# A graph network kernel in which each node's edge from itself is no longer gathered

## The reference

```python
for l in range(3):                                    # block 0
    xr = jnp.einsum('nd,rde->rne', x, W_rel[l])       # a table: 8 rows for each node
    agg = jax.ops.segment_sum(xr[edge_type, src], dst, num_segments=N)
    x = jax.nn.relu(agg + x @ W_root[l] + bias[l])
h = x @ Wv + bv                                       # block 1
q, k = h @ wq + bq, h @ wk + bk
e = q[src] + k[dst]
c = jnp.where(e > 0, e, 0.2 * e)
attn = softmax of c over the edges of each dst
out = jax.ops.segment_sum(h[src] * attn[:, None], dst, num_segments=n)
```

## Time and profile before

| | |
|---|---|
| median of 3 runs | 4654.57 us (4651.98 to 4656.97) |
| the profiled execution's own time | 4648.88 us |
| its span, first to last instruction | 4647.1 us |
| TensorE matmul busy | 3549.5 us, 76% |
| GpSimd busy | 3227.2 us, 69% |
| ScalarE busy | 1997.3 us, 43% |
| VectorE busy | 1198.7 us, 26% |
| indirect DMAs | 3328 = 4 x 832 |

### The profile page before, as it was taken

The page is one execution under the profiler, slowest core; times in us unless marked ns, Lnnn a source line. Parts: engine busy times, 40 slices in busy tenths (PEclk is TensorE's granted clock), DMA queues, the critical chain, the costliest instruction groups (busy, mean ns, idle before and its releaser), DMA issues.

```text
span 4647.1 us, 52438 instructions
## 1 busy us (share of the span) xinstructions
PE 3549.5 (76%) x12856; PEld 2444.5 (53%) x12856; DVE 1198.7 (26%) x3972; ACT 1997.3 (43%) x5249; POOL 3227.2 (69%) x3465
## 2 busy tenths in 40 slices
PE   9997888888887888888887666666664777777767
PEld 4444655555554555555554444444443665656656
DVE  2330000000000000000000111111112777777776
ACT  2334545454443444445453434434342444444444
POOL 1126777777775777777775777777776777777775
PEclk9998999999998999899998888888877888888888
DMA  5445545454544444444443444444443444444443
GB/s 201 183 176 162 166 156 166 156 167 156 163 160 137 160 151 159 151 152 158 150 159 122 119 116 117 118 116 118 117 118 97 112 114 113 114 113 113 113 113 88
DMA packets 233747, 643.65 MB, mean 139 GB/s; under 512 B 61158, under 2 KB 106663, under 8 KB 215028
## 3 DMA queue, kind: packets, MB, share of 16 engines
q0 software_dynamic: 160336, 439.40, 33.3%
q10 hardware_dynamic: 43128, 128.52, 7.5%
q1 hardware_dynamic: 29996, 72.34, 4.3%
HBM read 466.54 MB, written 173.49 MB: 138 GB/s over the span
## 4 chain that ended last, share of the span: by engine, by line
POOL 67%; issue 22%; PE 10%; DMA 1%; DVE 0%; SPq 0%; ACT 0%; ACTq 0%; DVEq 0%; POOLq 0%
POOL ring L482 67%; PE bank L1217 8%; DMA ring<-table,code 1%; PE sum_ps L1301 0%; PE sum_ps L1421 0%; PE turn_ps L1206 0%; DMA table<-stage 0%; DMA bias_row<-in_L_gnn_bias_dram 0%; PE bank L1377 0%; DVE stage L652 0%; DMA ring<-h_table,code 0%; PE bank L1371 0%; DVE masks L880 0%; DMA h_table<-stage 0%; SPq L532 0%
## 5 line engine op out<-in xcount | busy, mean ns | idle before, releaser
L482 POOL DMA_INDIRECT ring<-table,code x2496 | 2367.5, 949 | 861.6 <-issue 787.1
L1301 PE MATMUL sum_ps<-ring,masks 128*128 x5586 | 1531.3, 429 | 711.2 <-SPq L592 661.7
L1301 PEld LDWEIGHTS sum_ps<-ring,masks 128*128 128x128 f32 x5586 | 1148.7, 213 | 1058.2 <-issue 890.7
L1217 PE MATMUL bank<-wide,xT 128*128 128x512 f32 (+1 forms) x2744 | 1141.2, 570 | 9.3 <-DMA bias_row<-in_L_gnn_bias_dram 4.4
L482 POOL DMA_INDIRECT ring<-h_table,code x832 | 791.8, 952 | 272.3 <-issue 272.3
L1069 ACT ACTIVATE masks<-node_row,local 128x128 f32<-128x128 f32 x2793 | 830.8, 387 | 22.7 <-issue 13.2
L1217 PEld LDWEIGHTS bank<-wide,xT 128*128 128x128 f32 x2744 | 527.5, 194 | 573.9 <-issue 553.7
L979 ACT COPY stage<-bank 128x512 f32<-128x512 f32 x441 | 256.8, 583 | 953.5 <-PE bank L1217 953.3
L1421 PE MATMUL sum_ps<-ring,stage 128*128 x1862 | 505.6, 420 | 0.1
L970 ACT ACTIVATE xT<-turn_ps 128x256 f32<-128x256 f32 x196 | 75.4, 385 | 815.2 <-PE turn_ps L1206 812.3
L1421 PEld LDWEIGHTS sum_ps<-ring,stage 128*128 128x128 f32 x1862 | 382.0, 217 | 52.1 <-issue 0.5
(11 more groups left out here) (141 smaller groups left out, 1454.6 us busy)
## 6 DMA issues: line engine op xcount, KB each, us to landing
table<-stage ACTq DMA_DIRECT2D x96, 1024.0 KB, 4.5
table<-stage SPq DMA_DIRECT2D x48, 1024.0 KB, 4.1
ring<-table,code POOLq DMA_INDIRECT x2496, 2.8
ring<-h_table,code POOLq DMA_INDIRECT x832, 2.8
h_table<-stage ACTq DMA_DIRECT2D x49, 130.0 KB, 2.4
features<-xT SPq DMA_DIRECT2D x49, 128.0 KB, 4.0
first_T<-features ACTq DMA_DIRECT2D x49, 128.0 KB, 4.7
wide<-in_L_gnn_W_rel_dram SPq DMA_DIRECT2D x6, 1024.0 KB, 6.2
```

Of the source, the lines that this page charges most:

```text
L482: pool.indirect_dma_start(slot(c % RING, width), None, table, bass.IndirectOffsetOnAxis(ap=code[:, c:c + 1], axis=0)).then_inc(landed[n % ...
L1217: last = nc.tensor.matmul(bank[q][:, 0:width], xT[:, b, k, :], weights[:, k, 512 * q:512 * q + width], start=(k == 0), stop=(k == K - 1))
L1301: last = nc.tensor.matmul(sum_ps[b][:, 0:D], masks[:, b, s, :], at_offset(slots[s]), start=(s == 0 and l > 0), stop=(s == SLOTS - 1))
```

## The change

**The list.** The edges are laid out as 128 runs of 832, one in each partition. VectorE finds in each run the last loop of each node, takes it out, and closes the gaps: each kept edge is packed into one word with the number of places that it must move, and six steps `move_up` move words by 1, 2, 4, ... 32 places. Each run keeps 792 places, so the list has 792 chunks where it had 832, and a tile reads 18 gathered slots. The kept lists go to DRAM and come back as chunks. The loops' types are drawn out of each run by seven steps `take_loops` (8 at a time), and put in order by 56 small matmuls after the last tile of the stage.

With the reference's inputs a run keeps at most 787 edges, and has at most 52 loops (56 fit). The tiles' edges lie in at most 18 chunks, so the general path is not taken. Tile 47 begins at chunk 760; before, it began at chunk 798.

**Layers.** A node's loop adds the row of its own type from the table. The change adds it with VectorE, by 8 multiply-adds a tile, each with a 0 or 1 for each node. For layers 1 and 2 they read the PSUM banks right after `transform`. For layer 0 the tile's table rows (1 MB) are loaded back from DRAM.

**Attention.** The tile's own rows of `h_table` are loaded by a plain DMA (`own_rows`) and take the place of a 19th slot (`HELD` = 19).

```diff
+    RUN = -(-E // (16 * P)) * 16
+    KEPT = -(-(RUN - N // P + 5) // 8) * 8
+    NCH = KEPT
...
+    MEAN = -(-(E - N) * P // N)
     SLOTS = -(-(MEAN + P) // P) + 1
+    HELD = SLOTS + 1
...
+        FIRST_CLOSING = 4 if PAIRS >= 20 else 1
+        FIRST_STEP = 20 if PAIRS >= 20 else 2 * PAIRS
...
+        def place(after, half=0):
+            return min(FIRST_STEP + 2 * after + half, 2 * PAIRS)
...
             def evacuate(l, i, use, b, first=False):
                 q = R // 2 - 1
+                if not first:
+                    add_loops(l, i, use, b, range(0, R - 2))
                 dve.wait_ge(transformed[b], CREDIT + NB * use + q + 1)
                 dve.wait_ge(stored[b], table_stored(l, b, use))
                 nc.vector.tensor_copy(stage[:, b, 512 * q:512 * (q + 1)], bank[q][:, :]).then_inc(evacuated[q], 1)
...
+                add_loops(l, i, use, b, range(R - 2, R))
...
+            def add_loops(l, i, use, b, types):
+
+                for t in types:
+                    if t % 2 == 0 and t // 2 < R // 2 - 1:
+                        settle(dve, CREDIT + l * NT + i + 1)
+                        dve.wait_ge(evacuated[t // 2], CREDIT + l * NT + i + 1)
+                    if t:
+                        settle(dve, loops_done((l - 1) * NT + i, t))
+                        dve.wait_ge(root_step, loops_done((l - 1) * NT + i, t))
+                    nc.vector.scalar_tensor_tensor(root[:, i, :], bank[t // 2][:, t % 2 * D:(t % 2 + 1) * D], loop_weight(i, t),
+                                                   root[:, i, :] if t else bias_row[:, :], ALU.mult, ALU.add
+                                                   ).then_inc(root_step, 1)
+
+            def add_first_loops(i, j, b):
+
+                dve.wait_ge(back_loaded[b], 16 * (j + 1))
+                for t in range(R):
+                    if t:
+                        settle(dve, loops_done(i, t))
+                        dve.wait_ge(back_step, loops_done(i, t))
+                    nc.vector.scalar_tensor_tensor(root[:, i, :] if t == R - 1 else loop_ps, back[:, b, t * D:(t + 1) * D],
+                                                   loop_weight(i, t), loop_ps if t else root[:, i, :], ALU.mult, ALU.add
+                                                   ).then_inc(back_step, 1)
...
+            def load_back(i, b):
+                if not isinstance(i, int) or i > 1:
+                    settle(act, loops_done(i - 2, R))
+                    act.wait_ge(back_step, loops_done(i - 2, R))
+                act.dma_start(back[:, b, :], tables_by_node[0][bass.ds(i * P, P), :]).then_inc(back_loaded[b], 16)
...
+            def load_own(i, b):
+                act.dma_start(own_rows[:, b, :], h_table[bass.ds(i * P, P), :]).then_inc(own_loaded[b], 16)
...
             def transform(step, use, b, banks, first=False, lead=False, between=None):
...
                     pe.wait_ge(evacuated[q], CREDIT + step)
+                    if not first and q < R // 2 and not lead:
+                        pe.wait_ge(root_step, loops_done(step - NT - 1, 2 * q + 2))
...
             def next_table(l, i, j, b, upcoming=None):
 
+                if l == 0 and (not isinstance(i, int) or i < NT - 2):
+                    settle(pe, loops_done(i + 1, R))
+                    pe.wait_ge(back_step, loops_done(i + 1, R))
```

More of the change, by code:

```diff
@@ L60, in gnn_program, with slots_of, gathered @@
     RINGS_PAST = CH // RING
-    def slots_of(c):
-        return range(GROUP * c, min(GROUP * (c + 1), SLOTS))
+    def slots_of(c, end=HELD):
+        return range(GROUP * c, min(GROUP * (c + 1), end))
+    def gathered(c):
+        return slots_of(c, SLOTS)
     def uses(g):
@@ L397, in _ @@
             pool.wait_ge(ranges_ready, 2)
+            step(pool.tensor_scalar(most, most, -1.0, None, ALU.add))
             step(pool.tensor_tensor(meets, per_chunk(most), per_tile(tile_base[:, 0:NT]), ALU.subtract))
@@ L445, in _ @@
             pool.wait_ge(dst_ready, 2)
[L446 to L449 removed]
+            for first in range(0, NT, AT_ONCE):
+                end = min(first + AT_ONCE, NT)
+                _, begins = nc.values_load_multi_w_load_instructions(
+                    starts[0:1, first:end], engines=[pool.engine], min_val=0, max_val=CH - SLOTS,
+                    skip_runtime_bounds_check_because="first chunks, clamped where they are computed")
+                for i in range(first, end):
+                    pool.tensor_copy(local[:, i, 0:SLOTS], dst_T[:, bass.ds(begins[i - first], SLOTS)]
+                                     ).then_inc(prep_step, 1)
             steps[0] += NT
             pool.wait_ge(prep_step, steps[0])
[L452 to L453 removed]
+            step(pool.tensor_scalar(local[:, 0:NT, 0:SLOTS], local[:, 0:NT, 0:SLOTS], far_shift[:, 0:1], None, ALU.add))
+            step(pool.tensor_tensor(local[:, 0:NT, 0:SLOTS], local[:, 0:NT, 0:SLOTS],
                                     tile_base[:, 0:NT].unsqueeze(2).to_broadcast([P, NT, SLOTS]), ALU.subtract))
@@ new lines, in _ @@
+            takings = tuple(lambda k=k: take_loops(k) for k in range(LOOPS // 8))
+            before_layers_at(tile_before_layers, (
+                (SOME // 2 * 2, from_here_later), *((closing(k), step) for k, step in enumerate(closings)),
+                (place(0), chunk_ranges), (place(1), keep_code),
+                (place(1), count_below), *((place(2 + k // 2, k % 2), step) for k, step in enumerate(takings)),
+                (place(6), any_broken), (place(7), read_loops), (place(10), plan_sums)))
@@ L1180, in attend @@
                         exponentials(b, c)
+                    if c == 1 and not last and store:
+                        settle(act, pieces_done(L, i - 1))
+                        act.wait_ge(added, pieces_done(L, i - 1))
+                        load_own(i + 1, 1 - b)
                     if c >= 2:
@@ L1207, in turn, with transform @@
                 last.then_inc(turned[b], 1)
-            def transform(step, use, b, banks, first=False, between=None):
+            def transform(step, use, b, banks, first=False, lead=False, between=None):
                 found = None
```

407 lines of the change are left out of this document (293 added, 114 removed).

## The result

The changed kernel took **4587.44 us** (median of 4 runs, 4580.98 to 4592.06), the kernel before 4653.66 in the same session: ratio 0.9859, 95% interval [0.9847, 0.9871]. It is faster, by 1.4% and not by 4.0, and 4587 lies outside the forecast range. The profiled execution took 4585.81 us, its span is 4584.1.

A forecast was written before the change was run, and what follows sets the result against it. GpSimd's own gather pace was taken as the bound. Span: 4647.1 - 200.7 (gathers) + 1 (transfers) - 1.2 (gaps) + 15 (preparation) = 4461 us; adding 1.8 and 5.7 gave 4468 us, -4.0%, range 4452 to 4500.

The forecast's parts named there:

- Can the others follow?: Layers and attention: other engines keep up with 20.3 us a tile; in attention VectorE needs 15.2 and waited 4.2.
- The plan's own term: Preparation: L448's 57.8 us shrink to 25, from 49 copies and 7 loads of 1.5; cost nothing.
- attention does not follow: Rival, attention: a chain from largest score to weights and back keeps the tile at 21.3 us; 4518 us, chance 5%.
- Gathers removed: All four passes: 40 of 832 gathers fewer in each, 160 x 1.2546 us, -200.7 us.
- VectorE and TensorE in the layers: Pass 0: VectorE 9.8 us and TensorE 17.4 us a tile fit into 20.3; the adds cost TensorE nothing.
- TensorE's bank waiting for the adds: Sign of a wrong forecast: TensorE's first bank is held until VectorE's adds are over; no size given.
- Stage before the layers, +15: Before the layers: preparation steps over 2.4 us ahead of the norm hold TensorE's turn, +15 us, bounds 8 to 34.
- The plan ready in time: Before the first gather: the plan is ready some 34 us before the table is stored, so it costs nothing.
- Gaps, -1.2: Three gaps between passes: two slots of 0.43 us drop out, up to 0.5 us of late copies enter; -0.4 each.
- The gaps start from the same place: Ends of passes: the last chunk tile 47 needs is the 13th from the end in both lists.
- The last 32.04 us stay: After the last gather: the time stays 32.04 us, since attention keeps 19 slots.
- The rule weighed there: Layer 0: VectorE instructions with two SBUF inputs contend with GpSimd's SBUF reads; up to 21 us; milder contention rival, 4489.

The follow-up runs named there:

- with the load repaired: The changed kernel with plan rows 24 words apart in place of 23 and all 24 words loaded: 4476.34 us, ratio 0.9622.

## Why the prediction was wrong

- **The step that failed** is "Can the others follow?", its line on attention. I took VectorE's 740.53 us as 15.2 a tile, set 20.3 beside it, and wrote of the 4.2 us of waiting that "one microsecond less is there to take". The register load stood in no term of the sum, and it went from 1.60 to 5.15 us in three tiles of four. That a row shrinks from 96 to 92 bytes follows from the diff (`SLOTS`, with `PLAN = SLOTS + PIECES` in the kernel), and the 1.60 us were in the trace of before; what a start off 16 bytes costs was in no row of it. (The plan's own term does price such loads, seven of GpSimd's at 1.5 us; they took 1.61 in the median.) Nor were the 4.2 us all spare. Against them the loop had to take 1.0 us from the shorter gathers and 3.55 from the load, 4.55 in all, which would miss by 0.35 us a tile; the tiles came out at 22.4 us on the mean, 2.1 above 20.3. VectorE's loop without the slow load is 23.7 - 3.55 = 20.15 us (worked out), so before it had 21.3 - 20.15 = 1.15 us to spare and not 4.2: where no row is late, VectorE waits for ScalarE instead (136.1 us for 22.6). The pass came out 108 us above the forecast.
- **The rival that came true in name** was "attention does not follow" at 5%. Its mechanism, a chain that stays at 21.3 us, was not what happened, and its bound was wrong: I let the pass keep its length at worst, and it grew by 58 us, because the loop itself grew. The loop of 20.15 us fits into 20.3 with next to nothing spare, as the first repair (rows of 24 words, 23 loaded) shows.
- **Gathers removed**: right. Interval 1.25 us, 950 and 957 ns, and with the load repaired the four passes took 994.39, 988.54, 992.13 and 998.28 us, where "about 991" was said; attention's stayed 7 us above. What the load of the table rows took of pass 0 (1 us said) was not separated; that pass is 6 and 2 us longer than the other two.
- **VectorE and TensorE in the layers**: right in what they cost. The window of pass 0 gave VectorE 441.03 us of 975, 9.2 a tile where 9.8 was said, and TensorE 17.8 where 17.4 was. With adds narrowed or not, the passes stay. One sign that the prediction had named for being wrong, TensorE's bank waiting for the adds, does stand in the profile of the changed kernel, and it is the register load again: in all 39 cases TensorE's own load (5.4 us, in two of them 3.9) is over only 0.17 us before the matmul, as in the second and third line here, and with loads of 1.6 us (the run with 24 words loaded, last line) 3.2 us remain.

```profile
PE bank L1497 <- DVE root L781: 78.0, 39, 2.8
498.62 2.05 PE L1497 MATMUL bank<-wide,xT 128*128 128x512 f32 x2 [2.50 <-DVE root L781]
L334 PEldq TENSOR_LOAD <-plan x1: 5444/5444/5444, 493.0 to 493.0; - x1
PE bank L1500 <- DVE root L784: 3.2, 2, 1.7
```

- **Stage before the layers, +15**: 17.7 measured. The mechanism (a step over 2.4 us ahead of the norm holds the turn) was right; moving the steps behind the norm gave back 17.5 (384.62 to 367.08). The prices of the forms that the trace of before lacked came out close, except the scan, 1.88 us:

```profile
L889 DVE MAX8 loop_code<-masks 128x8 f32<-128x832 f32 x7 | 7.1, 1019 | 0.0
...
L891 DVE MATCH_REPLACE8 masks<-loop_code,masks 128x832 f32<-128x832 f32 x6 | 6.0, 1008 | 0.0
...
L867 DVE TENSOR_SCALAR masks<-masks 128x832 int32<-128x832 int32 x6 | 3.5, 586 | 0.0
L832 DVE TENSOR_TENSOR_SCAN masks<-masks 128x832 f32<-128x832 f32 x1 | 1.9, 1883 | 0.0
```

- **The plan ready in time**: right, its lead was 38.91 us (34 said).
- **Gaps, -1.2**: +1.7 measured. The first gap grew by 2.2. A likely reason, which no run tried by itself: TensorE now reaches the end of pass 0 later against the gathers. Before, the last tile but one's bank copy started 3.5 us before the last gather, with the load repaired 0.6 us before it (1378.38 against 1379.01). "The gaps start from the same place" left out that a tile of TensorE's work (17.8 us) now stands beside 20.3 and not 21.3.
- **The last 32.04 us stay**: 35.65 measured, 34.81 with the load repaired. What the remaining 2.8 us are was not tried.
- **Sum without the load**: 4476.3 with it repaired, against the 4468 forecast, 8 us off. A part of this closeness is luck: the trace's span is 4474.6 against the 4461 forecast, so the other terms together were 13 us off, and the 5.7 us by which the median was to lie above the profiled execution did not come (here they are the same).
- **The rule weighed there**: the Trainium skill ("SBUF — State Buffer", Who interferes with whom) would have made up to 21 us of the adds in layer 0. The first add of each eight, the only kind with both inputs in SBUF, went from 485 to 225 ns when narrowed, 49 x 0.26 = 12.7 us in all, and pass 0 from 994.39 to 993.07 us. So the traces do not agree with a cost of that size; one of 1.3 us could not be told from the scatter of pass 0 between runs with full adds (992.32 to 996.37).

## What to carry to other kernels

Busy time and waits between busy instructions do not show what a sequencer does between them. Waiting in a loop is not all spare time: when one wait goes, another can take its place. Where a loop is within a few us of the bound, read the code between two instructions of its timeline and look up every register load there by its source line; a wait put down to a semaphore whose data had long come is the sign. When a change alters the size of a table that is loaded row by row into registers, keep each row's start on a multiple of 16 bytes, and where it can be done, load whole groups of four words. A step that stalls a neighbour may need no speeding up, only a place in the order where its engine is idle anyway.

## What the runs showed of the hardware

- The price of loading words from SBUF into registers depends on where the first one lies (multiples of 16 bytes are counted from the start of the table; row 0 was fast in every run). Medians, from the lists of such loads by line:

| words, start | VectorE us | TensorE us | a word, VectorE |
|---|---|---|---|
| 24, on 16 bytes | 1.60 | 1.62 | 0.067 |
| 23, on 16 bytes | 2.05 | 2.09 | 0.089 |
| 24, off | 5.37 | 5.67 | 0.224 |
| 23, off | 5.15 | 5.44 | 0.224 |

Worked out from these: a group of four costs 1.60 / 6 = 0.27 us and a single word 0.224, so 23 words should take 5 x 0.27 + 3 x 0.224 = 2.01, and did take 2.05. A start 8 bytes off is as slow as one that is 4 bytes off (5.38 us on VectorE's odd tiles with rows of 26 words). That groups are what the engine does inside is argued from these sums, not seen. The Trainium skill ("Runtime: NRT & Kernel Launch", Instruction fetch mechanics) puts the loading of registers from HBM at about 200 ns a register. Here they come from SBUF: the loads off 16 bytes are near that figure, with 224 on VectorE, and those on 16 bytes far below it, with 67 to 89.
- The take-the-8-largest and the match-and-replace took 1.02 and 1.01 us over 832 elements, what a two-input form takes there; the running sum took 1.88.
